# Linear attention without a projection of values, and a residual that is added by identity products on TensorE and written back by ScalarE

## The reference

```python
# layer 0: softmax attention over 4096 tokens, 4 heads of 32
x = x + _L0_conv_ref(_gn(x), w_qkv, w_out, b_out)
t = _to_tokens(x)
# layer 1: linear attention, then a mixture of 8 experts, 2 for each token
t = t + _L1_attn_ref(_ln_t(t), W_qkv, W_out, b_out, gn_w, gn_b)
t = t + _L1_ffn_ref(_ln_t(t), router_w, router_b, expert_w, expert_b)

def _L1_attn_ref(x, ...):
    q, k, v = split(W_qkv @ x)                  # each (heads, d, tokens)
    q = softmax(q, over d) * scale
    k = softmax(k, over tokens)
    context = einsum('bhcj,bhdj->bhcd', k, v)   # (d x d) for each head
    out = einsum('bhcd,bhdi->bhci', context, q)
    out = W_out @ out + b_out
    out = (out - mean) * rsqrt(var + EPS) * gn_w + gn_b    # over channels and tokens
```

## Time and profile before

| | |
|---|---|
| median of 3 runs | 3132.67 us (3129.98 to 3133.64) |
| the profiled execution | 3128.74 us, span 3126.9 us |
| mean granted clock of TensorE | 0.961 |
| TensorE busy | 93% of the span |
| VectorE busy | 82% |
| ScalarE busy | 78% |
| GpSimd busy | 22% |

### The profile page before, as it was taken

The page is one execution under the profiler, slowest core; times in us unless marked ns, Lnnn a source line. Parts: engine busy times, 40 slices in busy tenths (PEclk is TensorE's granted clock), DMA queues, the critical chain, the costliest instruction groups (busy, mean ns, idle before and its releaser), DMA issues.

```text
span 3126.9 us, 62137 instructions
## 1 busy us (share of the span) xinstructions
PE 2902.8 (93%) x20368; PEld 1024.5 (33%) x20368; DVE 2573.8 (82%) x3652; ACT 2434.3 (78%) x3196; POOL 698.4 (22%) x726
## 2 busy tenths in 40 slices
PE   6999999978799999997979999999788999999978
PEld 3222222375322222237532222223743222222474
DVE  4888888878688888887868888888786888888877
ACT  4999999744599999974469999997446999999734
POOL 1112221114212212211421221121152122122115
PEclk8999999989899999998989999999898999999989
DMA  2555555500155565540025556554001555555300
GB/s 84 111 114 109 110 109 108 95 1 16 55 109 109 113 115 111 98 92 1 21 62 110 109 110 115 101 109 82 1 22 41 111 111 111 109 106 111 68 1 28
DMA packets 72168, 257.86 MB, mean 82 GB/s; under 512 B 8160, under 2 KB 10240, under 8 KB 71808
## 3 DMA queue, kind: packets, MB, share of 16 engines
q0 software_dynamic: 64512, 234.91, 39.8%
q1 hardware_dynamic: 7296, 18.51, 1.6%
HBM read 10.12 MB, written 8.39 MB: 6 GB/s over the span
## 4 chain that ended last, share of the span: by engine, by line
PE 77%; issue 10%; DVE 6%; DMA 2%; ACT 2%; POOL 1%; SPq 0%; ACTq 0%; DVEq 0%; POOLq 0%
PE BK L1032 76%; DMA RM<-EA 2%; DVE X L1005 2%; ACT KE L534 1%; POOL KE L457 1%; PE BK L1037 1%; DVE ST L642 1%; ACT PVC L513 1%; DVE X L841 0%; ACT KE L547 0%; ACT XT L552 0%; DVE X L997 0%; DVE RU L635 0%; DVE RU L636 0%; DVE ST L681 0%
## 5 line engine op out<-in xcount | busy, mean ns | idle before, releaser
L812 DVE TENSOR_TENSOR XT<-XT,KE 128x512 f32<-128x512 f32 x1344 | 1567.2, 1225 | 193.5 <-ACT KE L534 193.5
L534 ACT ACTIVATE KE<-BK 128x512 f32<-128x512 f32 (+1 forms) x1536 | 1489.0, 1021 | 152.0 <-PE BK L1032 65.0
L1032 PE MATMUL BK<-Q,K 32*128 32x512 f32 x8192 | 1190.7, 651 | 25.5 <-issue 13.2
L1032 PE MATMUL BK<-KE,V 128*32 128x512 f32 x6144 | 818.5, 606 | 0.0
L416 POOL DMA_DIRECT2D RM<-EA x448 | 392.0, 929 | 1544.4 <-ACT EA L534 748.1
L1032 PEld LDWEIGHTS BK<-Q,K 32*128 32x128 f32 x8192 | 325.9, 185 | 897.9 <-ACT KE L534 636.9
L534 ACT ACTIVATE EA<-BK 128x512 f32<-128x512 f32 (+1 forms) x512 | 496.9, 1025 | 34.7 <-PE BK L1032 6.5
L1032 PEld LDWEIGHTS BK<-KE,V 128*32 128x32 f32 x6144 | 125.5, 108 | 580.4 <-ACT KE L534 503.6
L1032 PE MATMUL BK<-EA,V 128*32 128x512 f32 x2048 | 272.7, 604 | 0.0
L1032 PE MATMUL BK<-WEXP,XT 128*128 128x512 f32 x512 | 236.9, 609 | 16.4 <-DVE X L1005 16.4
L610 ACT ACTIVATE RM<-BK,GT 128x128 f32<-128x128 f32 x512 | 145.9, 368 | 136.0 <-PE BK L1032 136.0
(11 more groups left out here) (153 smaller groups left out, 1883.4 us busy)
## 6 DMA issues: line engine op xcount, KB each, us to landing
RM<-EA POOLq DMA_DIRECT2D x224, 768.0 KB, 6.7
RM<-EA POOLq DMA_DIRECT2D x224, 256.0 KB, 3.3
XN<-in_x SPq DMA_DIRECT2D x16, 512.0 KB, 5.8
out<-X SPq DMA_DIRECT2D x16, 512.0 KB, 2.9
WEXP<-in_L_ffn_expert_w SPq DMA_DIRECT2D x1, 512.0 KB, 6.9
CONST<-in_consts SPq DMA_DIRECT2D x1, 384.0 KB, 5.8
WQKV<-in_L_conv_w_qkv SPq DMA_DIRECT2D x1, 192.0 KB, 2.4
WQKV<-in_L_attn_W_qkv SPq DMA_DIRECT2D x1, 192.0 KB, 6.0
```

The costliest lines, as they stand in the source:

```text
L534: nc.scalar.activation(exps(jt, p), scored(c * T + jt, p).rearrange("p a n -> p (a n)"), ACT.Exp, scale=SCALE0).then_inc(s_exp, 1)
L812: v.tensor_tensor(acc, acc, exps(jt, p), ALU.add).then_inc(s_adds, 1)
L1032: return nc.tensor.matmul(o, lhsT, rhs, start=start, stop=stop, skip_group_check=shared)
```

## The change

**Values.** The products with the value weights, ScalarE's copies of them (`values1`) and the semaphores s_v1 and s_v1c go. The context is made in another order of multiplication: 32 products Z x KT (the normalised tokens against exp of the keys) give KZ = Z^T K, VectorE copies it to SBUF, and one 128-column product with the value weights makes the context from it. This product stands behind the second transposed query chunk. The products of the queries and the transposes of the keys wait for the keys' copy (s_k1c) instead of that of V.

**Residual.** Both times the output of a layer is added to X, TensorE first puts X into the bank by a 512-column product with the identity (`residual`), and the four products accumulate on it. ScalarE copies the bank to X. VectorE has only the statistics left. In layer 0 ScalarE copies chunks 0 to 6 ahead of the first `normed`, and chunk 7 behind the first half's keys. In layer 1 the identity products of chunks 0 to 6 stand ahead of the wait for AT2, that of chunk 7 directly ahead of its own products, and all eight copies stand ahead of `normed(1, 0)`. The one-column products move from bank 0 to bank 7. `merge` moves behind the first chunk's statistics.

```diff
@@ ScalarE
+                def onto_x(ready, done, chunks):
+                    for c in chunks:
+                        act.wait_ge(ready, b * NCH + c + 1)
+                        part = X[:, c * TPB:(c + 1) * TPB, :].rearrange("p t c -> p (t c)")
+                        nc.scalar.activation(part, BK[c], ACT.Copy).then_inc(done, 1)
...
-                def values1(c):
-                    act.wait_ge(s_v1, b * NCH + c + 1)
-                    nc.scalar.activation(V[:, c * TPB:(c + 1) * TPB, :].rearrange("p t c -> p (t c)"), BK[c],
-                                         ACT.Copy).then_inc(s_v1c, 1)
-
+                onto_x(s_y0, s_x0, range(NCH - 1))
                 for half in range(2):
                     chunks = range(half * HCH, (half + 1) * HCH)
                     normed(0, half)
                     for c in chunks:
                         keys(c)
                     if half == 0:
-                        for c in chunks:
-                            values1(c)
+                        onto_x(s_y0, s_x0, [NCH - 1])
...
-                for c in range(HCH, NCH):
-                    values1(c)
                 q_exponentials(range(HCH // 2, HCH))
...
+                onto_x(s_y2, s_x1, range(NCH))
                 normed(1, 0)
                 normed(1, 1)
@@ VectorE
                     for c in range(first, first + HCH):
-                        onto_x(ready, done, c)
-                        if c == 1 and ready is s_y0:
+                        if c == 2 and done is s_x0:
                             dve.wait_ge(s_zero, b + 1)
                             merge(b * NCH + NCH, 1, True)
                         if c > first:
...
-                dve.wait_ge(s_ctx, b * 2 + 1)
-                v.scalar_tensor_tensor(CTX[:, :], BK[0][:, 0:C], SMALL[:, 11:12], BLOCK,
+                dve.wait_ge(s_ctx, b * 3 + 1)
+                v.tensor_copy(KZ[:, :], BK[0][:, 0:C]).then_inc(s_kz, 1)
+                dve.wait_ge(s_ctx, b * 3 + 2)
+                v.scalar_tensor_tensor(CTX[:, :], BK[0][:, C:2 * C], SMALL[:, 11:12], BLOCK,
@@ TensorE
+                def residual(c):
+                    part = X[:, c * TPB:(c + 1) * TPB, :].rearrange("p t c -> p (t c)")
+                    mm(BK[c], IDENT, part, stop=False, shared=True)
+
                 def project(c):
+                    residual(c)
                     for t in range(c * TPB, (c + 1) * TPB):
-                        last = mm(BK[c][:, (t % TPB) * C:(t % TPB + 1) * C], Q[:, t * P:(t + 1) * P], WOUT0[:, :])
+                        last = mm(BK[c][:, (t % TPB) * C:(t % TPB + 1) * C], Q[:, t * P:(t + 1) * P], WOUT0[:, :],
+                                  start=False, shared=True)
                     last.then_inc(s_y0, 1)
...
-                    for c in chunks:
-                        pe.wait_ge(s_k1c, b * NCH + c + 1)
-                        token_major(c, WQKV1[:, 2 * C:3 * C], s_v1)
                     if half == 0:
                         for c in chunks:
-                            pe.wait_ge(s_v1c, b * NCH + c + 1)
+                            pe.wait_ge(s_k1c, b * NCH + c + 1)
                             token_major(c, WQKV1[:, 0:C], s_q1)
...
                     if c >= HCH:
-                        pe.wait_ge(s_v1c, b * NCH + c + 1)
+                        pe.wait_ge(s_k1c, b * NCH + c + 1)
...
-                    last = mm(BK[0][:, 0:C], KT[:, t * P:(t + 1) * P], V[:, t, :], start=(t == 0), stop=(t == T - 1))
+                    last = mm(BK[0][:, 0:C], Z[:, t * C:(t + 1) * C], KT[:, t * P:(t + 1) * P], start=(t == 0), stop=(t == T - 1))
                 last.then_inc(s_ctx, 1)
                 for i, c in enumerate(q_order):
+                    if i == 2:
+                        pe.wait_ge(s_kz, b + 1)
+                        mm(BK[0][:, C:2 * C], KZ[:, :], WQKV1[:, 2 * C:3 * C]).then_inc(s_ctx, 1)
                     if i == 4:
                         pe.wait_ge(s_at, b * 3 + 1)
-                        mm(BK[0][:, C:2 * C], CTX[:, :], WOUT1[:, :]).then_inc(s_ctx, 1)
+                        mm(BK[0][:, 2 * C:3 * C], CTX[:, :], WOUT1[:, :]).then_inc(s_ctx, 1)
...
+                for c in range(NCH - 1):
+                    residual(c)
                 pe.wait_ge(s_at, b * 3 + 3)
-                tiles(lambda t: QT[:, t * P:(t + 1) * P], lambda t: AT2[:, :], s_y2)
+                for c in range(NCH):
+                    if c == NCH - 1:
+                        residual(c)
+                    for t in range(c * TPB, (c + 1) * TPB):
+                        last = mm(BK[c][:, (t % TPB) * C:(t % TPB + 1) * C], QT[:, t * P:(t + 1) * P], AT2[:, :],
+                                  start=False, shared=True)
+                    last.then_inc(s_y2, 1)
```

More of the change, by code:

```diff
@@ L199, in hybrid_kernel @@
         QSUM = sb("QSUM", [P, T * H])
+        KZ = sb("KZ", [P, C])
         CTX = sb("CTX", [P, C])
@@ L272, in hybrid_kernel @@
         s_k1e = sem("s_k1e")
-        s_v1 = sem("s_v1")
-        s_v1c = sem("s_v1c")
         s_q1 = sem("s_q1")
@@ L282, in hybrid_kernel @@
         s_ctx = sem("s_ctx")
+        s_kz = sem("s_kz")
         s_at = sem("s_at")
@@ L834, in _, with statistics_and_normed @@
                 mix_link, mix_n = chain(s_mix, b * MIX_LINKS)
-                dve.wait_ge(s_bias, b * 4 + 4)
-                def onto_x(ready, done, c):
-                    dve.wait_ge(ready, b * NCH + c + 1)
-                    part = X[:, c * TPB:(c + 1) * TPB, :].rearrange("p t c -> p (t c)")
-                    v.tensor_tensor(part, BK[c], part, ALU.add).then_inc(done, 1)
-                def onto_x_and_normed(ready, done, half):
+                def statistics_and_normed(done, half):
                     first = half * HCH
                     for c in range(first, first + HCH):
-                        onto_x(ready, done, c)
-                        if c == 1 and ready is s_y0:
+                        if c == 2 and done is s_x0:
                             dve.wait_ge(s_zero, b + 1)
@@ L855, in onto_x_and_normed @@
                     layernorm(mix_link, half, statistics(first + HCH - 1))
-                onto_x_and_normed(s_y0, s_x0, 0)
+                statistics_and_normed(s_x0, 0)
                 dve.sem_inc(s_smc, 1)
                 reciprocals(b * NCH + NCH, s_sum, SM)
-                onto_x_and_normed(s_y0, s_x0, 1)
+                statistics_and_normed(s_x0, 1)
                 def k_maxima(chunks):
@@ L900, in _ @@
                 mix_link(v.reciprocal(SMALL[:, 11:12], SMALL[:, 9:10]))
-                dve.wait_ge(s_ctx, b * 2 + 1)
-                v.scalar_tensor_tensor(CTX[:, :], BK[0][:, 0:C], SMALL[:, 11:12], BLOCK,
+                dve.wait_ge(s_ctx, b * 3 + 1)
+                v.tensor_copy(KZ[:, :], BK[0][:, 0:C]).then_inc(s_kz, 1)
+                dve.wait_ge(s_ctx, b * 3 + 2)
+                v.scalar_tensor_tensor(CTX[:, :], BK[0][:, C:2 * C], SMALL[:, 11:12], BLOCK,
                                        ALU.mult, ALU.mult).then_inc(s_at, 1)
                 q_summed(slice(HCH, NCH))
-                dve.wait_ge(s_ctx, b * 2 + 2)
-                v.scalar_tensor_tensor(AT[:, :], BO1[:, :], 1.0 / H, BK[0][:, C:2 * C],
+                dve.wait_ge(s_ctx, b * 3 + 3)
+                v.scalar_tensor_tensor(AT[:, :], BO1[:, :], 1.0 / H, BK[0][:, 2 * C:3 * C],
                                        ALU.mult, ALU.add).then_inc(s_at, 1)
@@ L918, in _ @@
                 dve.wait_ge(s_gst, b * 2 + 1)
-                mix_link(v.tensor_copy(SMALL[:, 0:1], BK[0][:, 0:1]))
+                mix_link(v.tensor_copy(SMALL[:, 0:1], BK[7][:, 0:1]))
                 mix_link(v.tensor_tensor(SMALL[:, 1:2], MV[:, 0:1], SMALL[:, 0:1], ALU.add))
@@ L923, in _ @@
                 dve.wait_ge(s_gst, b * 2 + 2)
-                mix_link(v.tensor_scalar(RA[:, 0:1], BK[0][:, 1:2], -1.0, 1e-5, ALU.mult, ALU.add))
+                mix_link(v.tensor_scalar(RA[:, 0:1], BK[7][:, 1:2], -1.0, 1e-5, ALU.mult, ALU.add))
                 rsqrt(mix_link, SMALL[:, 3:4], RA[:, 0:1], 1)
@@ L933, in _ @@
                 for half in range(2):
-                    onto_x_and_normed(s_y2, s_x1, half)
+                    statistics_and_normed(s_x1, half)
                 def over(x2):
@@ L1270, in _ @@
                 pe.wait_ge(s_bst, b * 2 + 1)
-                mm(BK[0][:, 0:1], NEG, MV[:, 0:1]).then_inc(s_gst, 1)
+                mm(BK[7][:, 0:1], NEG, MV[:, 0:1]).then_inc(s_gst, 1)
                 pe.wait_ge(s_bst, b * 2 + 2)
-                mm(BK[0][:, 1:2], NEG, SMALL[:, 2:3]).then_inc(s_gst, 1)
+                mm(BK[7][:, 1:2], NEG, SMALL[:, 2:3]).then_inc(s_gst, 1)
+                for c in range(NCH - 1):
+                    residual(c)
                 pe.wait_ge(s_at, b * 3 + 3)
-                tiles(lambda t: QT[:, t * P:(t + 1) * P], lambda t: AT2[:, :], s_y2)
+                for c in range(NCH):
[5 more added lines that the diff above has]
+                    last.then_inc(s_y2, 1)
                 for half in range(2):
```

## The result

The changed kernel takes 3140.03 us (median of 8 runs, 3134.97 to 3142.75) against 3132.40 us (median of 8 runs, 3127.79 to 3134.09): a ratio of 1.0025, with a 95% interval of 1.0014 to 1.0036. It is slower by 7.6 us.

A forecast was written before the change was run, and what follows sets the result against it. In layer 1's stretch no engine was full: VectorE, TensorE and ScalarE worked as a relay, each waiting for the one before. The legs came to -1.1 us a batch, -4.4 over four, median 3128.3 us, range 3115 to 3140.

The forecast's parts named there:

- leg 6: Third to fourth norm and out to the expert products: fourth norm 1.5 us earlier, 0.4 given back, leaving -1.1 a batch.
- the prices: Single operations in layer 1's stretch: 512-column product 0.86 us, ScalarE copy 0.60, VectorE addition 0.67.
- Legs 1 to 5: Layer 1 from attention's end to third norm; successive shifts -0.5, +1.5, -1.1, +0.1 and +0.9 us a batch.
- rival D: Identity products before AT2 run wholly at half clock: +3.3 us a batch, 3145.9 us; chance 0.12.
- Leg 2's half-clock term: Before the second norm, key products can fall on half clock: at most 1.2 us more, half of that taken.
- returning more than the legs gave: Named sign of error: TensorE's work from 714 us on starts in another clock state and gains extra; no size given.
- Sum. 4 x -1.1: All four batches' layer 1 stretches: -4.4 us in all, median 3128.3 us; chance 0.47.
- A: TensorE stays at full clock in the gap before AT2: -3.2 us a batch, 3119.9 us; chance 0.28.
- B: Value part pays in full, K's transposes ending 1.0 us sooner: 1.5 more a batch, 3122.3 us; chance 0.07.
- C: Transposes don't raise TensorE's clock, so K's transposes stay slow: 3.0 us more in all, 3131.3 us; chance 0.06.

The follow-up runs named there:

- e8: The kernel before with the value part alone, both residuals still added by VectorE: 3135.17 us, ratio 1.0012.
- e5: The changed kernel with router products of 128 columns instead of 8: 3125.04 us, 0.9977 of the kernel before.
- e14: Kernel before plus layer 1's residual and 128-column router products, first norm delayed 0.8 us a batch by repeated statistics: 3121.84 us.
- e17: As e14 but with the repeated statistics doubled, delaying the first norm by 1.7 us a batch: 3122.71 us.
- e18: As e14 but with the repeated statistics quadrupled, delaying the first norm by 3.4 us a batch: 3135.07 us.
- e13: e11 with four unused 512-column products where the first half's value products stood: 3121.76 us, 0.9966 of the kernel before.
- e4: The kernel before with the value part and layer 1's residual, without layer 0's: 3135.76 us, ratio 1.0010.
- e2: The kernel before with the residuals of layers 0 and 1, without the value part: 3134.78 us, ratio 1.0010.
- e6: The kernel before with layer 1's residual and router products of 128 columns: 3109.82 us, ratio 0.9929.
- e11: e6 with the value part added: 3122.74 us, 0.9970 of the kernel before.

## Why the prediction was wrong

Two steps of the forecast failed. The 0.4 us a batch that leg 6 gave back for the changing clock measured 2.9. And the sum took the legs as independent of each other, which the clock prevents. In what follows they are taken in their order.

**What bounds the kernel, and the prices: right.** The identity product took 0.86 us at full clock, the copies 0.60. ScalarE's copy being as cheap as VectorE's addition held: without its four additions the leg from the third to the fourth norm is 2.38 us shorter, and ScalarE's copies are not late for it. The rule of the Trainium skill (ScalarE: Activation LUTs, "Rules for kernel authors"), which sends additions to VectorE, is neither borne out nor refuted by that: the change puts a copy on ScalarE and the addition on TensorE.

**Legs 1 to 5: right in their order, with 1.7 us a batch missed by the fourth norm, most of it the clock's.** Norm, keys, context and the overrun of AT2 came nearly as worked out. The identity products ended at 691.24, which is 692.3 on the clock of the earlier trace rows, later than the forecast's 689.9. Most of that was handed down: AT2 itself was 2.3 late there. Their own length was 7.8 us against 7.5. So they ran partly at half clock, as forecast, and rival D (all at half clock) did not come about. Leg 2's half-clock term was 1.6 us in three batches and none in the third (17.73 against 16.13), where 0.5 had been taken and 1.2 allowed. An unforeseen 0.8 us came on the way to AT2, where the forecast had nothing: in the first batch the last eight transposes of the queries took 2.19 us from first to last instead of 1.73, and the products with AT behind them 8.09 instead of 7.31. e8, with the value part alone, has the same 0.8.

**Leg 6, "and out": the term that was most mis-sized.** "For this and the changing clock I give back 0.4": measured were 2.5 us to the first expert product and 0.4 more behind it. The place had been named among what would make the forecast wrong, but as a gain ("returning more than the legs gave"), and its price in the sum was far too low. The cause is shown by e5. With 8 columns each the second half's router products run at a clock of 0.50 in every batch of the changed kernel. With 128 columns they run at 1.00 in three batches of four, and the two legs are 4.3 us shorter where the rest of the batch is the same.

**The sum: the step that failed in kind.** "Sum. 4 x -1.1" takes each leg's change as if the others kept their lengths. The measured legs do add up to the batch, but e14, e17 and e18 show that a change in one of them changes the others: to 0.8, 1.7 and 3.4 us a batch the kernel answers 12, 13 and 25 us in all. A saving or a loss moves the later work, other work then falls on half clock, and that takes up or adds to the difference, so that a batch comes out near one of a few lengths. That the clock does it is shown in part: what changed between two such runs was read in their traces as work at 0.50 that came or went (e14, e17, e13, e5). Why the lengths lie 3.2 to 3.5 us apart is not shown and stays open. For the same reason the parts don't add. Their medians against before are +4 (values), +14 (layer 0) and -9 us (layer 1), where the legs had given -3, +5 and -6. Values and layer 1 together measured +3 (e4) where the single runs give -5, and layers 0 and 1 together +2 (e2) where they give +5. That all three add to +9 and the whole measured +7.6 is luck.

**The rivals.** A (full clock in the gap before AT2) did not come about in the changed kernel: 0.50 at 685.0 to 687.9 in the window above. It did in e6, though, with the same identity products: 1.00 throughout. In both, TensorE idles for the same 1.32 and 0.70 us ahead of the two one-column products. So the advice of the Trainium skill (TensorE: Matmul & The Clock Gate, "Why this matters for your kernels") against idle gaps between bursts of matmuls doesn't tell the two apart: one stayed at full clock and the other didn't. Why is not shown. B was wrong: the value part never paid (e8, e11). C is refuted again. In e6's first batch TensorE had idled for 3.5 us when the transposes of K began at 649.6, and nothing but these 32 transposes ran until 654.4. The windows of e6 in them:

```profile
650.00:652.00 2.00, 2.00 (x12) 2.00 (x11) 0.57 (x1) 2.00 (x5) 0.00 (x0) 0.50 0.00 0
652.50:654.50 2.00, 2.00 (x20) 2.00 (x19) 0.70 (x2) 2.00 (x5) 2.00 (x2) 1.00 0.00 0
```

The clock rose from 0.50 to 1.00 meanwhile. The rule in "Part 4: PE-mode transpose" of the same page of the Trainium skill (TensorE: Matmul & The Clock Gate) disagrees with that, and the trace decides. D was wrong in its place, but the outcome had its sign: the forecast gave a loss 0.15, and too little of it to the clock elsewhere.

The experiments point to a better kernel than either: layer 1's residual and wide router products, 3109.8 us, 0.71% faster than before, without the value part and without layer 0's residual.

## What to carry to other kernels

Where a stage of small products sits between idle stretches, read the granted clock of every stretch before and after the edit, in all repetitions, and price it as part of the change: removing work from TensorE can cost more than it saves. Here the value part took about 7 us of products a batch off TensorE and made the kernel 4 us slower. Where a row of products streams very few columns, try them wider: the 16 router products took 6.99 us with 8 columns at half clock, so about 3.5 at full clock (an estimate), and 3.84 with 128 columns at full clock. Before trusting a gain or loss under 1% in a loop like this one, shift the stage by a small delay: if the answer is out of proportion, one measurement tells on which step the kernel stands and little about the edit.

## What the runs showed of the hardware

TensorE at a granted clock of 0.50 through 12.5 us in which it was busy for 11.65 us (708.5 to 721.0, changed kernel), with router products of 8 columns and transposes; at 1.00 through the same stage, busy 10.14 of 13.0 us, with 128 columns (e5, first batch). Products of 128 columns at 0.50 all the same, from 710.3 to 713.7 (e6). A float32 router product took 0.44 us with 8 columns at half clock (6.99 / 16) and 0.22 with 128 columns at full clock ((3.84 - 0.27) / 16). The clock rose from 0.50 to 1.00 while TensorE did nothing but float32 transposes (e6, 649.6 to 654.4). The time of one batch took only values near 771.4, 774.9, 778.1 and 781.6 us in 54 cases, within 1.3 us of them.
